# Message products of a graph kernel with the operands of the TensorE changed over

## The reference, cut to what matters

```python
# layer 0
h = maximum(layernorm(x), 0)
deg = clip(sum(adj, axis=2), 1.0, None)
x = x + (adj / deg) @ h
# layer 1: thin out each node's neighbors by their rank, sort the neighbors' features,
# take three weighted quantiles of them, add them to the node's own, then a two-layer MLP
h = maximum(layernorm(x), 0)
x = x + L1_gnn(h, adj, nodemask, W1, b1, W2, b2)
```

## Time and profile before

| | |
|---|---|
| median of three runs | 1401.79 us (1400.84 to 1404.13) |
| the profiled execution's own time | 1393.88 us |
| its span | 1392.0 us |
| PE busy | 1196.3 us, 86% |
| DVE busy | 1128.0 us, 81% |
| ACT busy | 934.8 us, 67% |
| POOL busy | 708.3 us, 51% |
| mean granted clock of TensorE | 0.92 of full speed |

### The profile page before, as it was taken

How to read it: one execution, slowest core, us unless ns; L and a number is a source line. 1 busy time by engine, 2 the same in 40 slices (tenths; PEclk the granted TensorE clock), 3 DMA queues, 4 the chain that set the end, 5 groups by cost and what they waited for, 6 DMA issues and landing times. The chain is left out here.

```text
span 1392.0 us, 32405 instructions
## 1 busy us (share of the span) xinstructions
PE 1196.3 (86%) x12833; PEld 882.8 (63%) x12833; DVE 1128.0 (81%) x2092; ACT 934.8 (67%) x1691; POOL 708.3 (51%) x988
## 2 busy tenths in 40 slices
PE   4879999999898999889979989899899988687451
PEld 4758676867676776567757657667667766464320
DVE  3442499998998889888998979999899999989950
ACT  1787788786778687767758768686767878533310
POOL 0463354454268645765365744685357554704025
PEclk9988999999999999899998999999999999998655
DMA  4446454645144443435244432436144321420000
GB/s 138 133 153 195 142 163 123 199 136 185 49 155 156 148 127 110 139 112 181 96 140 129 128 108 100 156 127 211 33 157 160 122 86 36 149 64 32 1 8 15
DMA packets 119033, 167.09 MB, mean 120 GB/s; under 512 B 58816, under 2 KB 59472, under 8 KB 118864
## 3 DMA queue, kind: packets, MB, share of 16 engines
q1 hardware_dynamic: 103168, 117.72, 28.6%
q0 software_dynamic: 14336, 46.42, 8.7%
q10 hardware_dynamic: 1360, 0.74, 0.2%
HBM read 114.25 MB, written 50.59 MB: 118 GB/s over the span
## 5 line engine op out<-in xcount | busy, mean ns | idle before, releaser
L535 PE MATMUL psL<-H0A,AT 128*128 128x65 f32 x2048 | 261.5, 287 | 17.1 <-issue 9.7
L535 PEld LDWEIGHTS psL<-H0A,AT 128*128 128x128 f32 x2048 | 252.5, 203 | 27.1 <-issue 23.3
L1471 POOL DMA_INDIRECT rows<-VR,IDX x128 | 173.5, 1356 | 81.4 <-ACT JUNK L851 51.9
L1241 DVE TENSOR_TENSOR HUB<-HUB 128x1472 f32<-128x1472 f32 (+6 forms) x224 | 182.1, 813 | 9.0 <-ACT HUB L953 6.3
L1242 DVE TENSOR_TENSOR HUB<-HUB 128x1472 f32<-128x1472 f32 (+6 forms) x224 | 187.9, 839 | 0.0
L546 PE MATMUL psT<-UM,NEIT 128*128 128x512 f16 (+3 forms) x1024 | 164.7, 312 | 25.4 <-ACT VR L819 12.8
L638 PE MATMUL psG<-OHB,HL 128*64 128x384 f16 (+5 forms) x2048 | 172.9, 319 | 10.8 <-DVE OHB L1176 8.3
L845 ACT ACTIVATE VR<-psT 128x512 f16<-128x512 f32 x256 | 147.3, 598 | 50.9 <-PE psT L574 42.8
L1512 POOL DMA_INDIRECT out<-FR x128 | 149.4, 1167 | 37.5 <-issue 36.5
L629 PE MATMUL psG<-OHB,HL 128*64 128x256 f16 (+1 forms) x2560 | 154.6, 280 | 0.1
L953 ACT ACTIVATE HUB<-HUB 128x1472 f32<-128x1472 f32 (+5 forms) x168 | 90.5, 539 | 88.5 <-DVE HUB L1242 86.4
(11 more groups left out here) (134 smaller groups left out, 2218.3 us busy)
## 6 DMA issues: line engine op xcount, KB each, us to landing
AT<-in_adjt SPq DMA_DIRECT2D x128, 512.0 KB, 4.6
RR<-rows SPq DMA_DIRECT2D x128, 288.0 KB
FR<-rows SPq DMA_DIRECT2D x16, 272.0 KB, 4.9
X<-in_x SPq DMA_DIRECT2D x16, 256.0 KB, 3.6
h<-VR SPq DMA_DIRECT2D x16, 256.0 KB, 4.7
rows<-VR,IDX POOLq DMA_INDIRECT x128, 4.4
out<-FR POOLq DMA_INDIRECT x128
CH<-in_ch ACTq DMA_DIRECT2D x1, 192.0 KB, 4.3
```

Source lines behind the costliest of these rows:

```text
L535: m = e.matmul(ps["L"][:, 65 * t:65 * t + 65], AT[:, n % RING, kk, t * P:t * P + P], H0A[:, T * b + 2 * kp + kk, :], start=(kp == kk == t ...
L1241: e.tensor_tensor(b0, a0, a1, ALU.max)
L1471: e.indirect_dma_start(row_d[:, :], bass.IndirectOffsetOnAxis(ap=IDX[:, gb % 2, t:t + 1], axis=0), VR[:, t, :].bitcast(I32), None).then_in ...
```

## The change

A message step was eight products (two blocks of 128 sending nodes, four of 128 receiving ones), with a 128 x 128 block of adjacency as weights and the 65 feature columns moving. It becomes two: the 65 feature columns are the weights, and 512 adjacency columns move. The sums then lie the other way round in the bank, features on 65 partitions and 512 nodes along the free axis. So each half gets a new step, "lt", taken by the letter R ahead of "res": ACT copies the bank into a new SBUF tile `LT` (`messages_out`), and PE turns it back by four products with the identity (`messages_down`), into the same bank and the same layout as before. `result` waits for that (`p_lt`) in place of `p_msg`. `ORDER` is a new string, 32 letters longer, and the SBUF space set aside for POOL's DMA descriptors is 4096 bytes per partition instead of the default 16384, which makes room for `LT` (2 KB per partition).

```diff
 ORDER = (
-    "XnnnUUUAAAMMWUUMMARUADDMADUUDAADWMDDDDTUMDDDDDAUMBDDDDURMUMBBMNBrrTANBBABBAMrNUUgUrWrrrrhsscksssAAAl"
+    "XnnUUUnMMAAAUUMWUMAURRDDDDDMDDAADDTUMMMURAAAWURADDDDDDDDDNBMTBUUBBBBMMMrrAAgUBUBrrrNrrrssckNUssssssR"
...
             add("W", "off", g, b, hf)
+            add("R", "lt", g, b, hf)
             add("R", "res", g, b, 4 * hf)
...
+        LT = sb("LT", [P, 512])
...
                 for kk in range(2):
-                    for t in range(4):
-                        m = e.matmul(ps["L"][:, 65 * t:65 * t + 65], AT[:, n % RING, kk, t * P:t * P + P],
-                                     H0A[:, T * b + 2 * kp + kk, :], start=(kp == kk == t == 0),
-                                     stop=(kp == 3 and kk == 1 and t == 3), skip_group_check=True)
+                    m = e.matmul(ps["L"][0:65, :], H0A[:, T * b + 2 * kp + kk, :], AT[:, n % RING, kk, 0:512],
+                                 start=(kp == kk == 0), stop=(kp == 3 and kk == 1), skip_group_check=True)
                 m.then_inc(p_msg, 1)
+
+            def messages_down(g, b, hf):
+                w.wait_ge(a_lt, nth["lt", g, b, hf] + 1)
+                for t in range(4):
+                    m = e.matmul(ps["L"][:, 65 * t:65 * t + 65], LT[0:65, t * P:t * P + P], idf[0:65, 0:65],
+                                 start=(t == 0), stop=(t == 3), skip_group_check=True)
+                m.then_inc(p_lt, 1)
...
+            def messages_out(g, b, hf):
+                w.wait_ge(p_msg, nth["msg", g, b, hf, 3] + 1)
+                if nth["lt", g, b, hf]:
+                    w.wait_ge(p_lt, nth["lt", g, b, hf])
+                e.activation(LT[0:65, :], ps["L"][0:65, :], ACT.Copy).then_inc(a_lt, 1)
...
-                w.wait_ge(p_msg, nth["msg", g, b, t0 // 4, 3] + 1)
+                w.wait_ge(p_lt, nth["lt", g, b, t0 // 4] + 1)
...
-    nc = bacc.Bacc("TRN2", target_bir_lowering=False, num_devices=1)
+    nc = bacc.Bacc("TRN2", target_bir_lowering=False, num_devices=1, dynamic_dma_scratch_size=4096)
```

More of the change, by code:

```diff
@@ new lines @@
+    "cccSAWSSSsssRMcsssDUscsSccSSSAAAWDDMMDMDRhRDDDDlDDNDNDDDDXDNnUDUnUAnMMUhTMBAATMBBBBUBWfBBgrrrrrrrrAs"
+    "sUcUkssslcsssRSccssSSscSSsssccARMUssMMAAAcSSSDLLUDDDDDDMURWFFFDDDDDDLLRUAMNAFFFNLMDVNDDLUDDTFFTFMMBB"
+    "ddfmmVddBBrrgmmBBReehddBBmlLLrrrFvFmrrersssssssscddWFkmmccsssdUdAsscemcdvsmdcSSmSASAessdmccRKKKKUUDK"
+    "KMUDeSDDSDAAAoLLSSMMMKKmKKWRRDDDDDDDdDDFFFmDDDQDTeTBdtdLLmBBmBBBBBQQNdFFQQdUQQXrmrrrrmrrrFNssssssssU"
+    "edgNnsLLfsdUFAncAmnkmAeeFFddMMcLMccLcssssUstttWsUccMcmmQQRttFFFSQQAdSSSSSSStRdUmAADDDDDDMmDLLUtUttFF"
@@ new lines @@
+    "FLLeMMMFFFQAAWUDDDDdDDDLLFdtFFmmReeTLLhDDtlRDDddtTFFFQQfmmBUUBBBBBAABBdgdeMNGGVLmMmtdrrrrrUMrrJrdmNN"
+    "kssssLJssJJUWJeAcMQtmQccsstcddssmmQQReSAASSsSssddRQtttcUMttctQQhttttUsstttsUQMMMccAAeAmmdQVQRSQFQDQl"
+    "SSSDFFQRXQdQmNavQQDDeQmdWNDDDQQNdQDDDDDDDDDQnQEmmdeEEnUeADDLLUUnmdTGMBUBBBAMTKKKmBBBBrrrUddEKKKMEEFm"
+    "FWrrgFGrrmreAvEEoUEddkKKssstssssssLLFFFccEAAAmQLLmeeEKKMccQQddsssstsmmQcQRSSStScctDDDDssRFUttcMdtFFS"
+    "UAAMDeMDDSSSWUDDDDtDDMQDttDDUUdDDmmdQTRdTatBBBBmmRLFLFFBBBBMMALLMFUtFFhrrQQAULLrrrrrrOsstQQeessAsssF"
@@ new lines @@
+    "FAlQFgUssssLLtssJJJJFFJNddOmQQmccFNeddkccLNhMmmsddLAssmSSmQttSSRcWttRDQDDtDcMQlctQUeddeUctMAAAMMtStt"
+    "ttmmSQSSRtttDDQdQDfeWdVmQRDDdQQUmFFFfNQdQXAmQDDQUUdVQNLLQDDTeDBmDDNADDndTgQQnmnBBQQABBFmBBvQrrrQQQBE"
+    "rFMMMrrrrkddEFeEsstssssssessKsKKKKKKUKssLLKsccmmeWGGdEccEEdAUcsmmvMdccdsKmmeeEEUddFFFSSSmmSUcttSLSLS"
+    "SAARRDDDDMtDDDUdFFFoMEEttLLAAdDDFMEtQFFMQQLLtRWDDDDQQtTemmDUQQtDDDDFFFUUQQRddLTmLmBMMABMhtBBBBalgBBA"
+    "AFFFrreQQUNMWUULLOrrrrrrQteNssddsttsskcJQQmssmtcNsssssdsdcchtssJJJOJsmemdFFFQQAldtSemmSSSQQdRtdttmme"
@@ new lines @@
+    "AccDReMfcAcDUUSSddttDDttttSSfMMMQLLtAAtRtDDDQQDDQQWDDDDRQQNQmNdDmeDTDDQDTdFQQUUNQBBBBBBBXAABgFFrUQQr"
+    "mdQmmrVQQVdrQLLrrrmArFFQQsskFsEsseWsssLnsssddmmnncvceccKKKMMLeEEMdKdmssUUUmcdvdAMKSKSSSmKmoReeRGKKKU"
+    "DDssstDDSGMMFFFLQAddcLtmAAcUEtFEEFFAtmdteDcdMMSSStWEEmmEtERDDDDUDDEDDLLdDtdtFeUFmmFQQtUDDLLDDTQRQhFF"
+    "FQQMBBtQQlMQTQrrAAAMgQBBBBBBLLFNUUUrrrrrrtQQFFAMAtssssssNtsssseNsdWcdOmmtcssddLLOJsJJJhkcSmamRcceJSS"
+    "SeQQsstQQDddRttFtMttUctUDDDmmQAAccFSdMdFDtMttASSSMtmmttUUtRQQWeDDddQQQDDRDDDDlNQLLDmAQQQXNdemTeDDQND"
@@ new lines @@
+    "DQfdQQBTFQQFFULLQmmfBBBBBrFFFLQQddQAELmmrrBBrrrrrVEEeedssndEmgsmnddVcsesssssssnGmKKKGKkKKmvAcccMMUUd"
+    "dsssKMMKccctAUmmRSSSSeeFFFAUddtmWEsERvsMtStmDUDDDdLDLcdDDttAtSSSMFMAAWFFmmoMDDTUdLLtdEEEeQKKDDDDFeEF"
+    "FEQQRtQDBRUQADDUDLDLQQtBBBmmaQTQeAMtQQghBBBBMtQlrrrrrFFFNrrMrtUWkstsAssssssNLLsssAFFFtQQcNMJJJJddUUO"
+    "JssmmRttccLLcccsQQssddQQSSSSSSRMMQAmmhUUOetttttttttttcFlScSFddFMQQMfAtmmQQRQQAeDeDDADQddUQQmmReddWUQ"
+    "NmQDXdmNNDDLLQQDDDDDVQDfnFFFQQedQnVDLmmdLnDDDDFFTBUAAdTQQFmmdABBrBBEeevGMMdMgBtBBEEvLmmLrrrKKrrUrrss"
@@ new lines @@
+    "UUssssedmcdcmEKKssAKKAEEddssccKMFFFmWmReeGKKKLLddkocEEUssssQttccSSSSStmssmcSSSREeFFFtdtEMdDEALLDDmmt"
+    "DDDDMQQFMFFtUMAAQQUWtULLtDDDDDDQFFFQddUmmtRQLLQeeODTthFRFFQQAADDlJADDdTdMLLMQBBBBBBJJNJJmmQQWFFUUdBd"
+    "rgFrMmQQrrtrmrrBerttOkssddLesssAsssQQLmmtcNcctQtddtNssstMemmtUttQQacttdtssAedsSmfSSSssdtttmQmQAQRReQ"
+    "FQddUDDDQQDfMVKKFFQVUvmQKKQQAAccccLLKmQQDhSSSSDDDDKFFWQQMlQKQDDKDDvDdTEMKDDDDKTMdomRedemRmBBBBBBBBFd"
+    "dmmeLddrEEFrmmrrLtrrQrrgeettEEEGksscsEEtsssssNsEtENFFtsNEctcsssccQQtQtssccsddLQtmmcLGddFFSSSSSSSSQQF"
@@ L63 @@
+    "teQLQtLmQmQtdtFFFdtmmQtQthLLeeJFFFLJJLJJtFFFltQQQdtmdmQQtddtmOmQtdteeLdtLmmdtdOettmQQtmFFFQQdmQdffQQ"
+    "LQVdmQdeeQQKKLmQQdFQQmFVFQKvdQQamvQdmEdeeKLLmmoKddKFKFFeEmEmdmdmLeetQKLKttddEEEEEtmmEtFKtFFeLLQGQtQt"
+    "ddFFFmtdtQQttmQQQtdmmtQQeetQtJOtJJJJQGtQQQttQQttQttttQtttQEQQQQQQaQQQEQQQQQQQQEEEEEEOEEEEEOO"
 )
@@ L406, in program @@
         a_bat = sem("a_bat")
+        a_lt = sem("a_lt")
+        p_lt = sem("p_lt")
         (v_pad, v_mkf, v_mk, v_h0, v_h1, v_l, v_rem, v_lo, v_any, v_oh, v_wm, v_red, v_wz,
@@ L717, in tensor @@
                     w.wait_ge(v_mk, 1)
+                elif kind == "lt":
+                    messages_down(*a)
                 elif kind == "msg":
@@ L1016, in scalar @@
                     ranked(*a)
+                elif kind == "lt":
+                    messages_out(*a)
                 elif kind == "abs":
```

## The result

The changed kernel takes 1406.19 us (median of 17 runs, 1396.5 to 1410.76), the kernel before 1400.57 us (17 runs beside them). The ratio is 1.004, with a 95% interval from 1.0023 to 1.0057: slower by 5.6 us. Forecast were +15 us. The sign and the range held, the size did not. A few executions of a kernel are over 1.5% slower than its fastest; the ratios here leave them out, and they are three of e5's six, its traced one among them.

A forecast was written before the change was run, and what follows sets the result against it. PE was taken as the path up to 200 us, then PE and DVE in turn. On PE 32.7 - 9 + 6 - 10 = +20 us, of which +15 comes through: 1401.8 + 15 = 1417 us, range 1391 to 1438.

The forecast's parts named there:

- The turning: Turning the bank back on PE: 256 added instructions, 32.7 us, the main term (bounds 28.7 and 36).
- The waits at it: PE standing before the turning for ACT's copy: 7 of 32 halves, about 6 us (bounds 0 and 25).
- The loads: In message products on PE, weight loads set the old pace; with 512 columns, streaming replaces them and they are mostly hidden.
- The fourth rival: Loads of the new message products not covered: 56 us on PE, 44 us through, 1461 us; chance 0.03.
- What streaming saved: Message products on PE: 9 us of 261.5 won by 512 moving columns (bounds 30 won, 13 lost).
- The clock: PE's granted clock: streaming products raise and hold full clock, mostly loading ones don't; 10 us won (bounds 0 and 50).
- the new order: The order of steps with the new step added: costed at nothing, since every strand keeps its steps.
- The share itself: Share of added PE time reaching the kernel's time: all in the first stretch, 0.7 afterwards, 0.78 together.
- DVE's path: DVE bounds from 200 us on, only the first stretch shows, 5 us plus a few: 1407 us; chance 0.13.
- The clock's case: Streaming lifts most message stretches out of 1.2 GHz; PE wins 35 us, kernel at 1394 us; chance 0.24.
- The waits late in most halves: ACT's in-order list brings the copy late, 25 us on PE and rank copies held up: 1432 us; chance 0.12.
- The descriptor space: Smaller space costed at nothing; as a rival, POOL waits for scatter landings, 1460 us; chance 0.03.

The follow-up runs named there:

- e5: The changed kernel's new products, copy and turning in the old order, new step right ahead of the result's; 1.0552 of the kernel before.
- e13: The changed kernel in the old order, new step behind the second PE step after each half's fourth message step; 1.0329 of the kernel before.
- e7: The changed kernel without ACT's copy, PE turning a constant tile, message values not the reference's; 0.9958 of the kernel before.
- e9: The changed kernel measured again in a later set; 1.0032 of the kernel before.
- e1: PE alone on fixed tiles, old and new message products with pauses, nothing of the reference computed; old products stayed at 1.2 GHz, new ones reached 2.4 GHz after 3.7 us.
- e2: The old message products in the new order, nothing copied or turned back; 1.0117 of the kernel before.
- e3: The changed kernel without ACT's copy and without turning back, message values not the reference's; 0.9999 of the kernel before, 1402 us.
- e8: The kernel before with 4096 bytes of descriptor space alone; 0.9989 of the kernel before.
- e11: New products in the old order, nothing copied or turned, message values not the reference's; 0.9833 of the kernel before.
- e16: The changed kernel with neither copy nor turning, message values not the reference's, measured again in a later set; 0.9896 of the kernel before.
- e10: The changed kernel with each half turned back twice, 31 us more plain PE work; 1.0131 of the kernel before.
- e15: Old order, new products turned back by transposes, result's step at least two PE steps behind the turning in all but one half; 1.0229 of the kernel before.
- e12: The changed kernel turned back by transposes, with the new step's letter moved later in seven halves; 0.9997 of the kernel before.

## Why the prediction was right in its sign and wrong in its size

**The turning**, 32.7 us, measured 36.0 busy. Right.

**The waits at it**, 7 halves and 6 us, measured 7 times and 6.0 us. The numbers are right by luck. I had 4 halves with nothing in between and 3 with one step; in the trace the 4 wait 0.68 us each, those 3 don't wait, and the other 3.2 us stand in three halves with 4, 9 and 9 steps in between, where ACT came late. In e13, with two steps in every half, my rule has no wait at all, and there were 50 us. e7, without the copy, stands 0.7%, 11 us, under e9, which is of another set: so the copy may cost more than the idle time that it is named for.

**The loads**: they set the old pace, and with 512 columns they are hidden. Line 538's median is 592 ns, less the tail of 0.16 that is 0.43 us apiece, and in e1 PE is busy for 21.70 of 21.70 us with such products while 6.95 us of loads run beside them. The fourth rival is out. The Trainium skill's rule on loads of the same row group ("TensorE: Matmul & The Clock Gate", Part 3) doesn't hold for these products. What streaming saved: the messages' time at full-clock rate went from 250 - 34 / 2 = 233 us to 233 - 12 / 2 = 227 us, summed as above, 6 us where I said 9.

**The clock was sized too low.** I took 10 us of PE's time and had 0 to 50 as its bounds; it was 27 in the traced pair, 19 from e2 to e3, and 20 from e8 to e9 (184 to 144 us at half speed). The mechanism was the one that I named, and e1 shows it. I counted "a 20 us stretch's worth" of message runs, that is, only the messages' own slow time. But the clock is one for all products: in the traced pair 11 of the 27 us came back in the messages, (34 - 12) / 2, and 16 in the ranks, codes and gathers that run beside and behind them and inherit the clock. With 27 the sum on PE is 36 + 6 - 6 - 27 = +9, or 7 us by the share that I used, 0.27 + 0.73 x 0.7 = 0.78; with 20 it is +16, or 12 us. The clock alone thus doesn't bring the forecast to the measured 5.6.

**The step that failed is the one from PE's time to the kernel's.** I let 0.78 of the turning and its waits through, (32.7 + 6) x 0.78 = 30 us, and costed the new order at nothing. Neither holds. In us of the kernel's time, by the ratios:

| | forecast | e2, e3, changed | e11, e16, e9 |
|---|---|---|---|
| the new order | 0 | +16 | +9 |
| the products, with their clock | -15 | -16, new order | -24, old order |
| copy, turning and waits | +30 | +6 | +20 |
| all | +15 | +6 | +5 |

The forecast's 15 us for the products are (9 + 10) x 0.78. The middle column, from the runs whose kernel before takes what it takes beside the result, has the products as forecast. There the miss is the turning's price, 24 us too high, less the order's, 16 us too low. In the last column the two errors cancel and the products' larger gain is left. Each entry is uncertain by 4 to 9 us, each column joins two sets of runs, and which of the two describes the kernel stays open. In both, order and turning together cost less than 30 us, 22 and 29. That the turning is paid in two places, as a looser order and as work, fits this and isn't shown.

**The share itself**: plain work of PE came through by 0.5 to 0.6 (e9 to e10), less than the 0.78, though the runs leave up to 0.8.

**The rivals.** DVE's path had 1407 us, and 1406 were measured. That is chance as far as e9 and e10 tell: by that rival only the first stretch shows, and of the 26.1 us that e10's trace lies behind at 1150 us, 17.9 arose after 200 us. The clock's case had 35 us and the faster side; the truth lay between it and the forecast. The waits late in most halves are what e5 and e13 show for an order that isn't made for the step, 26 and 24 late copies. The descriptor space is out by e8. What stays open is how much of the new order's cost is the room for the turning and how much is chance. e13 to e15 show that two steps aren't enough in the old order, not that less than 0.6% would have bought the room.

## What to carry to other kernels

Where weight loads set TensorE's pace, turning the operands round saves little in the pace itself, but look at the granted clock: products that mostly load neither raised it nor held it across gaps, and the price falls on all products around them. Before adding a step between two engines in a kernel whose order is fixed, price the room that it needs in that order too, not only its work. Moving such a step later moves it on both engines, and in e12 that brought more waits, not fewer. And turn float32 back by a transpose, which is one instruction, in place of a product with the identity, which is two: that made this change a gain, 0.996 and 0.989 of before. In e12 the same transposes, placed later, came to 0.9997.
